# A graph network and a mixture of experts in one kernel: the first relation and the experts' lists reordered

## The reference, cut to what matters

```python
# third layer, every relation r: gather rows of x, then a product with W_rel[r] (768 x 768)
h1 = einsum('rni,rio->no', mean, W_rel) + x @ W_root + b_rgcn
# fourth layer
score = where(assigned, w_tok, -inf)                   # each token is assigned to 2 of 8 experts
order = argsort(-score, axis=1)[:, :capacity]          # an expert takes at most 196 tokens
dispatch = flat[order]
gate, up = silu(dispatch @ w1), dispatch @ w3
expert_out = ((gate * up) @ w2) * weight_sel
out = scatter_add(expert_out) + (silu(flat @ s1) * (flat @ s3)) @ s2
```

## Time and profile before

| | |
|---|---|
| profiled execution, its own time | 1431.91 us |
| its span | 1430.3 us |
| median of three runs | 1425.12 us |
| PE busy | 1311.4 us (92%) |
| DVE busy | 964.7 us (67%) |
| ACT, POOL busy | 556.2 us, 642.4 us |
| chain that ended last | PE 63%, DVE 24%, issue 5%, DMA 4% |
| matmuls of the relations, idle of PE before them | 1.0 us in all |

### The profile page before, as it was taken

How to read it: one execution, slowest core, us unless ns; L and a number is a source line. 1 busy time by engine, 2 the same in 40 slices (tenths; PEclk the granted TensorE clock), 3 DMA queues, 4 the chain that set the end, 5 groups by cost and what they waited for, 6 DMA issues and landing times.

```text
span 1430.3 us, 22837 instructions
## 1 busy us (share of the span) xinstructions
PE 1311.4 (92%) x7548; PEld 1114.4 (78%) x7548; DVE 964.7 (67%) x2158; ACT 556.2 (39%) x652; POOL 642.4 (45%) x564
## 2 busy tenths in 40 slices
PE   7988678899999979999999999999999769988997
PEld 5765578556997769999999999999867559765665
DVE  8967998878689645565666656565168765477634
ACT  1010575231432044545454545454157551212221
POOL 7025777777666533344344434443368720001112
PEclk9999688999999889999999999999999889988988
DMA  7950000020740338787878787878588843416745
GB/s 174 87 46 6 2 2 2 1 67 3 215 96 2 101 135 293 259 279 272 279 279 288 264 291 263 300 252 280 132 282 279 281 152 96 133 32 167 178 118 173
DMA packets 116403, 234.59 MB, mean 164 GB/s; under 512 B 36931, under 2 KB 57087, under 8 KB 116301
## 3 DMA queue, kind: packets, MB, share of 16 engines
q1 hardware_dynamic: 80780, 126.83, 31.0%
q0 software_dynamic: 22352, 70.40, 17.4%
q10 hardware_dynamic: 13200, 36.46, 6.9%
HBM read 195.26 MB, written 39.70 MB: 164 GB/s over the span
## 4 chain that ended last, share of the span: by engine, by line
PE 63%; DVE 24%; issue 5%; DMA 4%; ACT 3%; POOL 1%; another core or an unknown queue 0%; DVEq 0%; ACTq 0%; SPq 0%; POOLq 0%
PE PS L2722 30%; PE PS L2387 4%; PE PS L2712 3%; PE PS L3007 3%; PE PS L2598 3%; PE PS L2996 3%; DVE e L1320 3%; DVE mlo L2162 3%; PE PS L2855 2%; PE PS L2897 2%; PE PS L2785 2%; DVE e L1562 2%; DVE e L1599 2%; PE PS L2817 1%; PE PS L2906 1%
## 5 line engine op out<-in xcount | busy, mean ns | idle before, releaser
L814 POOL DMA_INDIRECT xg<-xn_dram,xrow x70 | 116.1, 1658 | 277.6 <-DVEq L1529 245.4
L2722 PE MATMUL PS<-whi,xhi 128*128 128x384 f32 x840 | 220.7, 343 | 1.0 <-ACTq L1102 1.0
L2722 PE MATMUL PS<-whi,xlo 128*128 128x384 f32 x840 | 214.7, 336 | 0.0
L2722 PE MATMUL PS<-wlo,xhi 128*128 128x384 f32 x840 | 213.1, 335 | 0.0
L1320 DVE TENSOR_TENSOR wlo<-raw,whi 128x2304 fp32r<-128x2304 f32 x68 | 175.2, 2576 | 38.0 <-ACTq L1085 31.5
L1083 ACT ACTIVATE whi<-raw 128x2304 fp32r<-128x2304 f32 x68 | 145.1, 2133 | 22.8 <-PE PS L2694 7.8
L2722 PEld LDWEIGHTS PS<-wlo,xhi 128*128 128x128 f32 x840 | 151.8, 188 | 0.0
L2722 PEld LDWEIGHTS PS<-whi,xlo 128*128 128x128 f32 x840 | 151.7, 188 | 0.0
L1320 DVE TENSOR_TENSOR xlo<-PS,xhi 128x768 fp32r<-128x768 f32 x70 | 67.0, 958 | 124.1 <-ACTq L1094 117.2
L2722 PEld LDWEIGHTS PS<-whi,xhi 128*128 128x128 f32 x840 | 148.3, 189 | 1.3 <-issue 1.3
L782 POOL DMA_INDIRECT evwb<-inv_dram,idxb x80 | 108.2, 1352 | 30.5 <-issue 22.4
(11 more groups left out here) (463 smaller groups left out, 2671.2 us busy)
## 6 DMA issues: line engine op xcount, KB each, us to landing
raw<-in_L_gnn_W_rel SPq DMA_DIRECT2D x68, 1152.0 KB
z_dram<-xn ACTq DMA_DIRECT2D x70, 384.0 KB, 7.3
gw<-in_L_gnn_W SPq DMA_DIRECT2D x2, 2304.0 KB, 27.4
fw<-in_L_ffn_w SPq DMA_DIRECT2D x8, 576.0 KB
fw<-in_L_ffn_w ACTq DMA_DIRECT2D x1, 4608.0 KB
y_dram<-yb ACTq DMA_DIRECT2D x14, 294.0 KB
xn_dram<-xn SPq DMA_DIRECT2D x10, 384.0 KB
wroot<-in_L_ffn_w SPq DMA_DIRECT2D x5, 576.0 KB, 5.0
```

The costliest lines, as they stand in the source:

```text
L814: pool.indirect_dma_start(xg[b][j][:, :], None, xn_dram, bass.IndirectOffsetOnAxis(ap=xrow[:, b, j:j + 1], axis=0)).then_inc(x_gathered[b] ...
L2722: mm = pe.matmul(slot(q)[:, s * BANK:s * BANK + HALF], a[:, k, :], wt[:, k, s * HALF:(s + 1) * HALF], start=(k == 0 and part == 0), stop=( ...
```

## The change

```diff
-SPREAD_AHEAD = 4
+SPREAD_AHEAD = 3
+X_SLOT = (0, 3)
+SHARED_SLOT = (0, 1, 2, 1, 2)
...   SyncE, before the loop that loads the weights of relations 1 to 33
+            sp.wait_ge(x_gathered[0][1], 16)
             with sp.Fori(1, REL) as r:
                 load_raw(r, False)
...   ScalarE: take_x reads columns2(X_SLOT[j]) instead of columns2(0)
+            def shared_out(t):
+                act.wait_ge(outer_full, t + 1)
+                step.do(act.activation(xn[:, t, :]..., slot(SHARED_SLOT[t])..., ACT.Copy))
+                act.sem_inc(outer_taken, 1)
             for t in range(LOGITS_WITH):
                 shared_gate(t)
+            act.activation(table_of_exp[:, :], ones[0:P, 0:1], ACT.Exp)
             shared_turned(0)
             router(2)
             shared_gate(3)
             shared_turned(1)
+            score_row(0)
+            act.wait_ge(xn_stored, 32 * T)
+            shared_out(0)
...   shared_out(1) to (3) between the other steps, then
             for j in range(RT):
                 take_x(0, j)
+            shared_out(4)
             for n in range(NE):
                 expert_gates(n)
...
+                if n == 0:
+                    score_row(2)
+                if n + SPREAD_AHEAD < NE:
+                    score_row(n + SPREAD_AHEAD)
+                elif FINAL - RT <= n < FINAL:
+                    hot_out(n - (FINAL - RT))
...
                 y_out(n, 0)
-                take_x(n + 1, 1)
...
+                for j in range(RT):
+                    take_x(n + 1, j)
                 y_out(n, 1)
...   VectorE, third layer: in_list(2, 0) goes ahead of the last layer norm
-            in_list(2, 0)
-            w_low(0, 0, 0, 1)
             for j in range(RT):
+                w_low(0, 0, j)
                 x_low(0, 0, j)
                 free_slot(j)
...   VectorE, fourth layer
             def add_shared(t):
-                dve.wait_ge(outer_full, t + 1)
...
+                dve.wait_ge(outer_taken, t + 1)
+                do(tt(x_res[:, t, :], xn[:, t, :], x_res[:, t, :], ALU.add))
...
             shared_hidden(3)
-            shared_hidden(4)
             dve.wait_ge(earlier_ready, 1)
             rank(0, 0, 3)
-            add_shared(0)
-            add_shared(1)
+            shared_hidden(4)
             rank(0, 3, T)
             placed(0)
...   then rows2(0), rank(1), placed(1), ident16, and in place of the old order
+            for n in range(NE):
+                hidden_rest(n)
+                if n + 1 < NE:
+                    rows2(n + 1)
+                hidden_first(n)
+                if n + 2 < NE:
+                    rank(n + 2, 0, T)
+                    placed(n + 2)
+                    if 0 < n:
+                        add_shared(n - 1)
+                elif n + 2 == NE:
+                    row_tables()
                     add_lower()
...
+            last_low(0)
             add_higher(0)
             add_higher(1)
-            last_low(0)
-            add_higher(2)
             last_low(1)
-            add_higher(3)
-            add_higher(4)
+            for t in range(2, T):
+                add_higher(t)
...   TensorE, relations
-                    pe.wait_ge(split_lo, at(i, b, 2, 2 + SPLITS1))
+                    pe.wait_ge(split_lo, at(i, b, 2, 1 + SPLITS1))     # and 2 + SPLITS1 at k == K // 2
-            for _ in range(6):
+            for _ in range(2):
                 pe.matmul(slot(0)[0:P, 0:HALF], xn[:, T - 1, 0:P], xn[:, T - 1, 0:HALF], start=True, stop=True)
...   TensorE, fourth layer: last_logits(), after shared_inner(2), becomes logits_alone(3) after shared_inner(1)
...   and logits_alone(4) after shared_inner(2)
...   turn_x writes slot(X_SLOT[j]); in place of its wait on x_taken
+                if j == 1 and e > NE - SPREAD_AHEAD:
+                    pe.wait_ge(hots_ready, e - (NE - SPREAD_AHEAD))
+                elif j == 1:
+                    pe.wait_ge(srow_ready, e + SPREAD_AHEAD if e else 2)
...   shared_outer(0, 0) and spread(3, row 0) now ahead of shared_inner(4), list_places(0) ahead of
...   score_spread(1), both turn_x(0, j) ahead of shared_outer(4, 2)
+            for e in range(NE):
+                def between():
+                    if e + 1 < NE:
+                        list_places(e + 1)
+                    if e == 0:
+                        score_spread(2)
+                inner_product(e, between)        # between() runs ahead of the third part, "up"
                 if e + SPREAD_AHEAD < NE:
                     score_spread(e + SPREAD_AHEAD)
+                elif e < FINAL:
                     turn_hots(e - (FINAL - RT))
+                outer_product(e, 0)
+                if e < FINAL:
+                    for j in range(RT):
+                        turn_x(e + 1, j)
                 outer_product(e, 1, 0 if e == FINAL else 2)
```

More of the change, by code:

```diff
@@ L1226, in take_x @@
                 act.wait_ge(turned, n * RT + j + 1)
-                step.do(act.activation(fxT[n % 2][:, :, j * HT:(j + 1) * HT], columns2(0)[:, :, 0:HT], ACT.Copy))
+                step.do(act.activation(fxT[n % 2][:, :, j * HT:(j + 1) * HT], columns2(X_SLOT[j])[:, :, 0:HT], ACT.Copy))
                 act.sem_inc(x_taken, 1)
@@ L1272, in shared_turned @@
                 act.sem_inc(hT_ready, 1)
+            def shared_out(t):
+                act.wait_ge(outer_full, t + 1)
+                step.do(act.activation(xn[:, t, :].rearrange("p (b c) -> p b c", b=2),
+                                       slot(SHARED_SLOT[t]).rearrange("p (b c) -> p b c", c=BANK)[0:P, :, 0:HALF], ACT.Copy))
+                act.sem_inc(outer_taken, 1)
             for t in range(LOGITS_WITH):
                 shared_gate(t)
+            act.activation(table_of_exp[:, :], ones[0:P, 0:1], ACT.Exp)
             shared_turned(0)
@@ L1993, in _ @@
             do(dve.memset(xn_all[96:128, :, :], 0.0))
+            in_list(2, 0)
             for t in range(T):
@@ L2293, in _ @@
             shared_hidden(3)
[L2294 removed]
             dve.wait_ge(earlier_ready, 1)
             rank(0, 0, 3)
[L2297 to L2298 removed]
+            shared_hidden(4)
             rank(0, 3, T)
             placed(0)
[L2301 removed]
             rows2(0)
[L2303 to L2307, removed]
[L2308 to L2338 removed]
+            rank(1, 0, T)
+            placed(1)
+            do(dve.tensor_copy(ident16[:, :], ident[0:P, 0:P]))
+            for n in range(NE):
[10 more added lines that the diff above has]
+                    row_tables()
+                    add_lower()
             def add_higher(t):
@@ L2716, in take_r, with relation_product @@
                 pe.wait_ge(free[q], at(i, b, 1, BEFORE["relations"][q]))
-            def relation_product(q, hi, lo, b, done):
+            def relation_product(q, hi, lo, b, done, second_half=None):
                 for k in range(K):
+                    if k == K // 2 and second_half is not None:
+                        pe.wait_ge(split_lo, second_half)
                     for part, (a, wt) in enumerate(((hi, whi[b]), (hi, wlo[b]), (lo, whi[b]))):
@@ L2908, in shared_inner, with logits_alone @@
                 mm.then_inc(inner_full, 1)
-            def last_logits():
+            def logits_alone(t):
                 pe.wait_ge(free[3], BEFORE["slot3"][3])
-                for t in range(LOGITS_WITH, T):
-                    pe.wait_ge(xT_ready, XT_TURNED[5] + t + 1)
-                    c = (t - LOGITS_WITH) * NE
-                    for k in range(K):
-                        mm = pe.matmul(slot(3)[0:P, c:c + NE], xT[:, k, t * P:(t + 1) * P], s13[:, k, 2 * F:2 * F + NE],
-                                       start=(k == 0), stop=(k == K - 1))
-                mm.then_inc(full[3], 1)
+                pe.wait_ge(xT_ready, XT_TURNED[5] + t + 1)
+                c = (t - LOGITS_WITH) * NE
+                for k in range(K):
+                    mm = pe.matmul(slot(3)[0:P, c:c + NE], xT[:, k, t * P:(t + 1) * P], s13[:, k, 2 * F:2 * F + NE],
+                                   start=(k == 0), stop=(k == K - 1))
+                if t == T - 1:
+                    mm.then_inc(full[3], 1)
             pe.wait_ge(split_lo, 2 * REL + SPLITS1 + K // 2)
```

85 lines of the change are left out of this document (13 added, 72 removed).

## The result

The changed kernel took 1447.28 us in the median of 4 runs (1444.02 to 1454.31), beside 1425.31 of the kernel before on the same chip: a ratio of 1.0169, with a 95% interval of 1.0128 to 1.021. So the change makes the kernel 18 to 24 us slower. The forecast was 1439, 13.6 us slower (a ratio of 1.0095), in the range 1418 to 1451: the sign is right, the size is 4 to 10 us too small.

What follows compares the result with a forecast made beforehand. The prediction took the 34 relations in steady state as bound by PE, so the change could act only at their start and in the fourth layer. Its terms, -4.0 - 2.5 + 7.1 + 8.4 + 6.0 - 1.4 = +13.6, gave 1439 us, range 1418 to 1451.

Steps and rivals of the forecast that it cites:

- Part 1: First relation: gathers issue and land earlier, first product begins 5.5 us earlier, less 1.5 for the low clock; -4.0 us.
- Part 2: Shared expert and start of expert 0: two `add_shared` no longer stand ahead of expert 0's list; -2.5 us.
- Part 3: Experts 0 to 4: PE waits 3.4 us for each second gather and loses 2.0 us of clock; +7.1 us.
- Rival (b): Experts 0 to 4: clock falls further, each wait costing 4 us instead of 2; +10, 1449 us; chance 0.12.
- Rival (a): Experts 0 to 4: gather and load share evenly, wait 1.9 us, clock holds; -10.3 instead of +7.1, 1421 us; chance 0.25.
- rival (a) with no wait at all: Experts 0 to 4: gathers cause no wait, 72.3 us for the five, 1412 us in all; chance 0.05.
- Part 4: Expert 5: `turn_hots(0)` waits for the eighth list, PE stands 10.1 us, then 3 us of low clock; +8.4 us.
- Part 5: Experts 6 and 7: `row_tables` comes later, PE waits about 5.5 us for expert 7's hidden product; +6.0 us.
- Part 6: Tail: `last_low(0)` ahead of the additions, joins start 6.0 us after the first outer product instead of 7.4; -1.4 us.

Runs made afterwards that it cites:

- e2: The whole change with its edits at the first relation taken back, so only the expert edits; 1442.69 us, ratio 1.0152 to the kernel before.
- e7: The whole change without SP's wait for the second gather ahead of the raw load of relation 1; 1451.93 us, ratio 1.016 to the kernel before.
- e12: e10 with each relation's list for the next but one placed between the weight split's halves on DVE; 1399.37 us, ratio 0.9788 to the kernel before.
- e10: e8, but weight loads of experts 3 to 7 wait for the inner product and then the gather's landing; 1400.02 us, ratio 0.9813 to the kernel before.
- e8: The whole change with the edits of e3, e4 and e5 together; 1414.16 us, ratio 0.993 to the kernel before.
- e5: The whole change with the five additions of the lower experts moved behind the last hidden product; 1441.17 us, ratio 1.0108 to the kernel before.
- e1: The kernel before with only the change's edits at the first relation; 1415.31 us, ratio 0.9952 to the kernel before.
- e3: The whole change with the transposes of the hot weights moved one expert later; 1421.90 us, ratio 1.0008 to the kernel before.
- e4: The whole change with weight loads of experts 3 to 7 released by the previous expert's outer product; 1428.93 us, ratio 1.005 to the kernel before.

## Why the prediction was right, and where it was short

The terms, as forecast, between the two profiles shown, and between means over all profiles that have the same code in the window (two for before, from 6 to 12 for after):

| part | forecast | two profiles | means |
|---|---|---|---|
| 1 first relation | -4.0 | -3.2 | -2.9 |
| 2 shared expert | -2.5 | -2.5 | -2.6 |
| 3 experts 0 to 4 | +7.1 | +10.1 | +6.1 |
| 4 expert 5 | +8.4 | +12.3 | +11.2 |
| 5 experts 6 and 7 | +6.0 | +7.6 | +7.6 |
| 6 tail | -1.4 | +2.4 | +2.5 |
| sum | +13.6 | +26.7 | +21.9 |

The sign came as forecast, and so did the places of the gain and of the waits; the sum is 8 us short, and part 6 has the wrong sign. The means sum to what the times show, 18 to 24 us. Between the two profiles the message stage takes 3.6 us off and the start 0.7, which leaves the 22.4 of the span.

**Part 1** was 1.1 us too large. The mechanism is shown: e2, where `w_low` runs beside the gathers again, issues them in 2.52 and 2.35 us, the change in 0.95 to 1.02. That it is `w_low` and not the load of the next weight shows in e7, where this load is issued ahead of the second gather again:

```profile
515.69 0.39 SPq L635 DMA_DIRECT2D raw<-in_L_gnn_W_rel  x1
515.97 1.02 POOL L817 DMA_INDIRECT xg<-xn_dram,xrow  x1 [22.39 <-DMA xn_dram<-xn]
517.30 0.97 POOL L817 DMA_INDIRECT xg<-xn_dram,xrow  x1 [0.30 <-issue]
```

The Trainium skill ("SBUF — State Buffer", section "Who interferes with whom") infers that descriptor generation goes on beside a `tensor_tensor`; by the measured issues it does not here. The first product begins 9.5 us after the last tile's transposes instead of 15.2, as forecast, and at full clock: the 1.5 us that I had taken off for the clock are not lost there. What failed is the sentence that the first product covers the late load. The weight is split in time, but the list for relation 3 stands on DVE behind both halves, and PE waits 2.8 to 3.9 us for it, with the lower clock behind; e12 shows it by taking the wait away. I had named what is queued behind the load on SP, not what is queued behind its consumers on DVE.

**Part 2** came out as forecast in size. No run has it alone, and the window that holds it lasted 97.4 to 102.6 us in the 14 profiles, so that a microsecond more or less isn't shown.

**Part 3** is right in the mean, in part by luck: an expert was to cost 14.3 + 3.4 + 2.0 us and cost 14.6 + 2.5 + 2.4, so that a wait taken too long made up for a clock priced too low. The place, the five waits and the missing ones in experts 5 and 6 are as forecast; the wait was 2.5 to 2.9 us in the profile shown. Rival (b), 4 us of clock, describes the profile shown, where the low clock reaches into the next inner product, and not the mean. That its time of 1449 is near the measured 1447.28 is owed to parts 4 to 6. Rival (a), the fair share, fell: the gather is used 7.5 us after its issue. The Trainium skill ("DMA: Bandwidth & Descriptors", section "Queues, rings and completion order") has the engines alternate between queues packet by packet; that doesn't keep a half tile from losing 3 us to a load of 1.15 MB here. By e10 the time that rival (a) with no wait at all named for these experts, 72.3 us, was there to be won (72.88), but only with the load behind the gather.

**Part 4** was 2.8 us too small. The stall was 10.28 us, forecast 10.1. The clock behind it is the larger part of the error, 4.3 in the mean for 3; and before, expert 5 took 18.1 in the mean of two profiles, 0.9 less than in the one I used.

**Part 5** was 1.6 us too small. PE waited 7.68 instead of 5.5 (my own terms, 20.0 less 14, made 6.0). From POOL's first issue to DVE's first addition it took 11.9 us (1410.42 to 1422.36), not the 10.6 of before; the chain of waits ends in the last of these gathers:

```profile
1415.46 6.79 DMA fx<-y_dram,yrow
```

**Part 6** failed in sign, and by most, 3.9 us. `last_low(0)` was in time, but I had priced the two outer products at full clock, behind a wait that I had forecast myself. They took 9.93 us instead of 5.91, and the joins follow at once. In e8, where PE hardly waits ahead of them (0.34 us), they take 5.91 and the joins begin 5.98 us after the first outer product, as forecast. The other four kernels with e5's edit have 6.5 to 7.6 us there, with a wait of PE for `last_low(0)` behind the additions.

So of the 8 us that were missing, some 5 are one step: the clock lost behind the two long waits, taken as 3 and 0 us and measured as 4.3 and 4. That step was in the sum for the short waits and dropped for the last.

## What to carry to other kernels

Price a wait of PE twice, once for itself and once for the products behind it at half the clock; here waits of 2.5 us cost 4.9 in the mean, and one of 7.7 cost 4 more in the two products behind it; a wait forecast in one part must carry its clock into the next. When a gather is moved close to its use, order the large loads behind its landing, not behind the instruction that frees their buffer; that separated 19.5 us an expert from 14.6. Before an operation is put ahead of others on an in-order engine, look at what its semaphore needs last: one group of transposes that asks for the eighth list cost 16 us, most of what the change lost.

## What the runs showed of the hardware

- Behind 24 of 30 waits of 1.9 to 3.6 us on PE the granted clock fell to its lower level, behind six it did not. With products without use in the gap it stayed at 1.00: 85.23 us for five experts against 93.94 to 102.24 without them.
- A gather of 98 rows is used 4.5 us after its issue alone and 7.5 us beside a load of 1.15 MB issued 0.6 us after it; a gather of 128 rows landed 5.7 us after its issue beside the load of a relation's weight (e7), and 4.4 to 4.8 without it (e1, e3, e4).
- Indirect gathers of 128 rows took POOL 2.52 and 2.35 us to issue while DVE ran `w_low` (e2), and 1.02 and 0.97 without it, though a weight's load had been issued ahead of them (e7).
- A stage whose code is the same in all kernels lasted 134.5 to 149.2 us. In this kernel a difference of less than 10 us between two profiled executions says nothing by its span; only windows cut around the edit do.
